# Dividing the attention heads by their softmax sums in the last stage instead of in the head loop, in a fused transformer layer

## What is computed

```
x = x + attention(layernorm(x))          # 16 heads of 64 columns, rotary keys and queries,
x = x + ffn(layernorm(x))                # keys multiplied by a 64x64 matrix a head

# attention, for each batch and each head
sim = q @ k'.T                           # 1024 x 1024
p   = exp(sim - rowmax(sim))
z   = (p @ v) / p.sum(axis=-1)           # the division that the change moves
out = concat(z) @ Wo

# ffn: layernorm, ternary-quantised 256->1024, exact gelu, layernorm, ternary-quantised 1024->256
```

## Time and profile before

| | us |
|---|---|
| median of 3 executions | 3566.96 |
| lowest and highest | 3565.94, 3568.25 |
| span of the profiled execution | 3566.5 |
| TensorE matmul busy | 3472.3 (97%) |
| VectorE busy | 2841.1 (80%) |
| ScalarE busy | 2283.5 (64%) |
| GpSimd busy | 2784.1 (78%) |

### The profile page before, as it was taken

How to read it: one execution, slowest core, us unless ns; L and a number is a source line. 1 busy time by engine, 2 the same in 40 slices (tenths; PEclk the granted TensorE clock), 3 DMA queues, 4 the chain that set the end, 5 groups by cost and what they waited for, 6 DMA issues and landing times. The chain is left out here.

```text
span 3566.5 us, 70837 instructions
## 1 busy us (share of the span) xinstructions
PE 3472.3 (97%) x21150; PEld 2250.9 (63%) x21150; DVE 2841.1 (80%) x4376; ACT 2283.5 (64%) x4340; POOL 2784.1 (78%) x1407
## 2 busy tenths in 40 slices
PE   6999999999999999999999999999999996999999
PEld 4656655665555556555565555566666663888888
DVE  6778777778777777777777777887777777899998
ACT  2666666666666666666666666666666664555555
POOL 2999999999998899999999998999999995222222
PEclk8999999999999999999999999999999998999999
DMA  5222222222222222322222222222222112333332
GB/s 197 84 82 104 88 82 79 78 103 87 87 85 102 85 87 83 106 87 85 82 105 87 87 84 101 87 87 87 104 77 75 59 62 88 92 97 96 97 95 69
DMA packets 219697, 321.71 MB, mean 90 GB/s; under 512 B 20832, under 2 KB 144224, under 8 KB 214880
## 3 DMA queue, kind: packets, MB, share of 16 engines
q1 hardware_dynamic: 210144, 309.28, 25.5%
q10 hardware_dynamic: 9216, 8.39, 0.7%
HBM read 186.52 MB, written 61.60 MB: 70 GB/s over the span
## 5 line engine op out<-in xcount | busy, mean ns | idle before, releaser
L422 POOL TENSOR_TENSOR prob_sum<-prob_sum,prob 128x1024 f32<-128x1024 f32 x762 | 1883.6, 2472 | 248.0 <-ACT prob L506 204.7
L506 ACT ACTIVATE prob<-scores 128x512 f32<-128x512 f32 x2048 | 1072.0, 600 | 572.6 <-PE scores L724 557.8
L654 DVE TENSOR_REDUCE row_max<-max_scores 128x1 f32<-128x512 f32 x1536 | 988.3, 685 | 285.7 <-PE max_scores L773 267.7
L910 PE MATMUL attn_out<-prob,v 128*64 128x512 f32 x4096 | 930.8, 596 | 0.0
L715 PE MATMUL scores<-q_hi,k_hi 64*128 64x512 f32 x2048 | 782.6, 415 | 7.0 <-ACT scores L477 3.9
L724 PE MATMUL scores<-q_lo,k_hi 64*128 64x512 f32 x2048 | 752.8, 393 | 1.3 <-issue 1.3
L720 PE MATMUL scores<-q_hi,k_lo 64*128 64x512 f32 x2048 | 753.5, 394 | 0.0
L910 PEld LDWEIGHTS attn_out<-prob,v 128*64 128x64 f32 x4096 | 285.0, 137 | 557.5 <-issue 556.6
L773 PE MATMUL max_scores<-k_hi,q_hi 64*128 64x512 f32 x1536 | 578.1, 429 | 7.2 <-DVE rows L644 3.0
L477 ACT ACTIVATE scores<-neg_max_seeds 128x512 f32<-128x512 f32 x1024 | 553.3, 603 | 7.6 <-DMA neg_max_seeds<-neg_max_halves 7.6
L715 PEld LDWEIGHTS scores<-q_hi,k_hi 64*128 64x128 f32 x2048 | 376.4, 185 | 275.3 <-issue 159.0
(11 more groups left out here) (137 smaller groups left out, 5005.7 us busy)
## 6 DMA issues: line engine op xcount, KB each, us to landing
rows<-rows SPq DMA_DIRECT2D x512, 128.0 KB, 2.0
neg_max_seeds<-neg_max_halves SPq DMA_DIRECT2D x128, 512.0 KB, 3.8
w_group<-w_parts SPq DMA_DIRECT2D x30, 1536.0 KB, 6.9
attn_normalised<-z_stage SPq DMA_DIRECT2D x128, 256.0 KB, 2.0
v<-attn_normalised SPq DMA_DIRECT2D x64, 512.0 KB, 4.1
x_turned_parts<-x_tile_parts SPq DMA_DIRECT2D x49, 256.0 KB, 3.0
xt_batch<-x_turned_parts SPq DMA_DIRECT2D x7, 1792.0 KB, 11.2
x_in<-in_x SPq DMA_DIRECT2D x64, 128.0 KB, 3.8
```

The lines of the kernel that those rows point to most:

```text
L422: nc.gpsimd.tensor_tensor(psums[half][:, :, :], a, prob[:, n % RING, :, :], ALU.add).then_inc(added, 1)
L506: nc.scalar.activation(prob[:, n % RING, e, :], S[e][n % 2][:, :], ACT.Exp).then_inc(exped[e], 1)
L654: nc.vector.reduce_max(mx[1 - u][:, e, n // 2, n % 2:n % 2 + 1], bank_of(e, jj)[:, :], axis=AX.X)\
L910: nc.tensor.matmul(O[rows(e), :], V[k // 2 % 2][:, j, col:col + DH], prob[:, n % RING, e, :], start=j == 0, stop=j == 7).then_inc(pv_made[ ...
```

## The change

The division leaves the attention loop. Halves of `attn_out` are stored as ScalarE has copied them. The sums are made once a pair, at the end of q = 0 of the next pair, by four products of 32 columns each (two halves, two heads) that fill the four quarters of partitions of `shared`. ScalarE copies the bank to SBUF, SP moves the four rows of 512 into 128x16, VectorE inverts these 2048 values, and SP stores them to HBM. Three `prob_sum` buffers are used in turn in place of two. In the last stage a new station NORM stands between LOAD and SPLIT: SP loads the inverses of the tile spread over 64 partitions for each head of a pair (two DMAs), and GpSimd multiplies the 128x1024 tile by them. The pipeline is one step longer. The diff, cut to its core:

```
-        psums = [sb(f"prob_sum{h}", [P, 2, HALF], F) for h in two]
+        psums = [sb(f"prob_sum{i}", [P, 2, HALF], F) for i in range(3)]
+        sum_rows = sb("sum_rows", [P, HALF], F)
+        sum_cols, inv = (sb(n, [P, 16], F) for n in ("sum_cols", "sum_inverted"))
+        def sums_of(k, half):
+            return psums[(2 * k + half) % 3][:, :, :]
...
         # SP
             def store_z(t, h):
-                wait(sp, z_made, 2 * t + h + 1)
+                wait(sp, z_copied, 2 * t + h + 1)
+            def sum_columns(t):
+                wait(sp, l_copied, t + 1)
+                at_rest()
+                wait(sp, inv_made, t)
+                at_rest()
+                sp.dma_start(sum_cols[:, :], sum_rows[0:P:32, :].rearrange("r (a c) -> r a c", c=16)).then_inc(l_in, 16)
+            def store_inverse(t):
+                wait(sp, inv_made, t + 1)
+                at_rest()
+                sp.dma_start(inv_scr[t].rearrange("h e (a c) -> (h e a) c", c=16), inv[:, :]).then_inc(inv_out, 16)
...
                     for c in two:
                         swap(Q, t, c)
+                if k >= 1:
+                    sum_columns(t - 1)
...
                     max_rows(t, 1)
+                if k >= 1:
+                    store_inverse(t - 1)
                 if attn:
                     store_z(t, 0)
...
             pairs(sp, span)
             store_z(T - 1, 1)
+            sum_columns(T - 1)
+            store_inverse(T - 1)
...
         # GpSimd
                 if j == 1:
-                    wait(pool, l_made, 4 * (t - 1) + 2 * half + 2)
+                    wait(pool, l_made, 4 * (t - 1) + 4 * half)
-            def norm_z(t, h):
-                wait(pool, inv_made, 2 * t + h + 1)
-                wait(pool, z_copied, 2 * t + h + 1)
-                nc.gpsimd.tensor_tensor(zst[h][:, :], zst[h][:, :], inv[:, :], ALU.mult).then_inc(z_made, 1)
-                        if jj == 0 and q == 1 and k >= 1:
-                            norm_z(t - 1, 1)
-                        if jj == 0 and q == 3 and attn:
-                            norm_z(t, 0)
...
         # ScalarE
+            def copy_sums(t):
+                wait(act, l_made, 4 * t + 4)
+                wait(act, l_in, 16 * t)
+                nc.scalar.activation(sum_rows[:, :], M[:, :], ACT.Copy).then_inc(l_copied, 1)
                     if attn and q < 3:
                         seed(t, q + 1)
+                    if q == 0 and k >= 1:
+                        copy_sums(t - 1)
...
         # VectorE
-            def invert(t, h):
-                wait(dve, l_made, 4 * t + 2 * h + 2)
-                wait(dve, z_made, 2 * t + h)
-                nc.vector.reciprocal(inv[:, :], M[:, :]).then_inc(inv_made, 1)
+            def invert(t):
+                wait(dve, l_in, 16 * (t + 1))
+                wait(dve, inv_out, 16 * t)
+                nc.vector.reciprocal(inv[:, :], sum_cols[:, :]).then_inc(inv_made, 1)
-                        if k >= 1:
-                            invert(t - 1, 1)
-                    if q == 2 and attn:
-                        invert(t, 0)
+                    if q == 2 and k >= 1:
+                        invert(t - 1)
...
         # TensorE; its waits on inv_made for the bank become waits on l_copied
-            def sums(t, h, last=False):
-                for e in two:
-                    if last and h:
-                        pe.wait_ge(added_last, 7)
-                    else:
-                        wait(pe, added, 14 * t + 7 * h + 7)
-                    nc.tensor.matmul(M[rows(e), :], ones[:, :], psums[h][:, e, :], start=True, stop=True).then_inc(l_made, 1)
+            def sums(k, t, last=False):
+                if last:
+                    wait(pe, added, 14 * t + 7)
+                    pe.wait_ge(added_last, 7)
+                else:
+                    wait(pe, added, 14 * t + 14)
+                for h in two:
+                    for e in two:
+                        i = 2 * h + e
+                        nc.tensor.matmul(M[32 * i:32 * i + 32, :], ones[:, 0:32], sums_of(k, h)[:, e, :], start=True, stop=True)\
+                            .then_inc(l_made, 1)
-                        if q == 2:
-                            ...
-                            sums(t, 0)
...
     # feed_forward
-        LOAD, SPLIT, Y_MADE, UP, GATE, DOWN, RES = range(7)
+        LOAD, NORM, SPLIT, Y_MADE, UP, GATE, DOWN, RES = range(8)
...
         # SP
                 if at(j, q, LOAD):
                     t, r = at(j, q, LOAD)
+                    wait(sp, z_normed, t - 1)
+                    sp.sem_inc(sp_carrier, 1)
+                    for e in two:
+                        sp.dma_start(zi[r % 2][e * DH:(e + 1) * DH, :, :],
+                                     iv[(t >> 3) & (B - 1), (t >> 2) & 1, e, :, bass.ds((t & 3) * P, P)].partition_broadcast(DH))\
+                            .then_inc(inv_in[r % 2], 16)
                     if q >= 2:
                         wait(sp, z_lo, t - 1)
...
         # GpSimd
-            pool.wait_ge(folded, 3)
             def step(j, q):
+                if q == Y_MADE:
+                    pool.wait_ge(folded, 3)
+                if at(j, q, NORM):
+                    t, r = at(j, q, NORM)
+                    pool.wait_ge(z_in[r % 2], 16 * (t >> 1) + FREE)
+                    pool.wait_ge(inv_in[r % 2], 32 * (t >> 1) + 32)
+                    nc.gpsimd.tensor_tensor(za[r % 2], za[r % 2], zi[r % 2][:, :, :], ALU.mult).then_inc(z_normed, 1)
                 if at(j, q, DOWN):
...
         # ScalarE
                 if at(j, q, SPLIT):
-                    act.wait_ge(z_in[r % 2], 16 * (t >> 1) + FREE)
+                    wait(act, z_normed, t + 1)
```

More of the change, by code:

```diff
@@ L176, in adds_by, with attention @@
     return 7 * (n // 8) + max(n % 8, 1)
-def attention(nc, x, xt_scr, w_scr, z_scr, nm_scr, w_out, late, late_in, stage, XT, W, V, WB, prob, space, ident, gam, alpha, ffn_in, ffn_parts, next_loads):
+def attention(nc, x, xt_scr, w_scr, z_scr, inv_scr, nm_scr, w_out, late, late_in, stage, XT, W, V, WB, prob, space, ident, gam, alpha, ffn_in, ffn_parts, next_loads):
     with ExitStack() as ctx:
@@ L270, in _ @@
         def _(sp):
-            for s in swap_in[K] + swap_in[Q] + z_stored + nm_in + nm_out + seed_in + [x_in] + x_stored:
+            for s in swap_in[K] + swap_in[Q] + z_stored + nm_in + nm_out + seed_in + [x_in, l_in, inv_out] + x_stored:
                 sp.sem_inc(s, CREDIT)
@@ L391, in _ @@
             store_z(T - 1, 1)
+            sum_columns(T - 1)
+            store_inverse(T - 1)
             for h in two:
                 wait(sp, z_stored[h], 16 * T)
+            wait(sp, inv_out, 16 * T)
             for u in two:
@@ L399, in _ @@
         def _(pool):
-            for s in rot_made + [added, z_made, x_rs]:
+            for s in rot_made + [added, x_rs]:
                 pool.sem_inc(s, CREDIT)
@@ L420, in add @@
                     wait(pool, added, 14 * t + adds_by(n - 1))
-                    a = psums[half][:, :, :]
-                nc.gpsimd.tensor_tensor(psums[half][:, :, :], a, prob[:, n % RING, :, :], ALU.add).then_inc(added, 1)
+                    a = sums_of(k, half)
+                nc.gpsimd.tensor_tensor(sums_of(k, half), a, prob[:, n % RING, :, :], ALU.add).then_inc(added, 1)
             def rope(t, x):
@@ L451, in _ @@
             pairs(pool, span)
-            norm_z(T - 1, 1)
         @blk.scalar
         def _(act):
-            for s in exped + hi_made + seeded + [v_copied, nm_hi, z_copied, x_normed, x_hi]:
+            for s in exped + hi_made + seeded + [v_copied, nm_hi, z_copied, l_copied, x_normed, x_hi]:
                 act.sem_inc(s, CREDIT)
@@ L550, in _ @@
             copy_z(T - 1, 1)
+            copy_sums(T - 1)
         @blk.vector
@@ L695, in _ @@
             pairs(dve, span)
-            invert(T - 1, 1)
+            invert(T - 1)
         @blk.tensor
@@ L755, in max_score @@
                     if q == 1 and i == 2:
-                        wait(pe, inv_made, 2 * (t - 1) + 2)
-                    if q == 3 and i == 2:
-                        wait(pe, inv_made, 2 * t + 1)
+                        wait(pe, l_copied, t)
                 elif q and i == 0:
@@ L888, in span @@
                                     wait(pe, x_red[1], 16 * (t + 1) + 2)
-                                wait(pe, inv_made, 2 * (t - 1) + 1)
-                            sums(t - 1, 1)
-                        if q == 2:
-                            if proj:
-                                wait(pe, v_copied, 2 * pp + 1)
-                            else:
-                                if prep:
-                                    wait(pe, x_red[1], 16 * (t + 1) + 10)
-                                wait(pe, inv_made, 2 * (t - 1) + 2)
-                            sums(t, 0)
+                                wait(pe, l_copied, t - 1)
+                            sums(k - 1, t - 1)
                         half = q // 2
```

(16 more changed lines are left out.)

12 lines of the change are left out of this document (7 added, 5 removed).

## The result

The changed kernel takes 3639.97 us (median of 4 runs, 3637.97 to 3643.01) against 3566.45 us before: a ratio of 1.0207, 95% interval 1.0192 to 1.0221. It is slower by 73.5 us; the forecast was 3634. The attention part became shorter, as forecast, and the last stage longer. But the last stage became so in two ways, and the prediction had seen one.

What follows compares the result with a forecast made beforehand. TensorE bounds the attention loop; in the last stage, delaying VectorE by more than 0.28 us lengthens the step. Sum: 3566.5 - 28 (loop) - 8 (way out) + 99 (last stage) + 4 (its start) = 3633.5, forecast 3634 us, range 3592 to 3695.

Steps and rivals of the forecast that it cites:

- q = 2 without sums, four products at once, another arrangement: Attention loop, TensorE: sums leaving q = 2 save 0.85 us a pair; four 32-column products run together, changing arrangement costs 0.1.
- Rival (a): Attention loop, q = 0: the four 32-column products run only two at a time, +53 us, 3687 us; chance 0.17.
- The collision of `q_lo`: Attention loop, q = 1: VectorE's `q_lo` waits behind GpSimd's next addition, ending 1.1 us later; 0.3 us a pair, +19 us.
- Until the last stage: Before the last stage: loop -28 us, last pair and way out -8, start of the last stage +4.
- the start of the stage: Last stage's start: the first two NORM fall among VectorE's ten `ln_shift_wide`; between nothing and 4.8 us, taken as +4.
- The term of +99 us for NORM: Last stage: GpSimd's NORM makes VectorE's `gelu_gained` wait, +1.65 us a step over some 60 steps.
- The rule of exclusion: Last stage: VectorE instructions with two SBUF inputs and GpSimd instructions reading SBUF exclude each other throughout; the same +99 us.
- rival (c): Last stage: GpSimd yields while running, VectorE waits only 0.5 to 1.2 us a step; 3565 to 3607 us; chance 0.09.
- issued ahead of the load, in SP's idle time: Last stage: SP issues the two DMAs of inverses before the load of `v`; no cost, DMA share some 0.5.
- the prediction's sign: Last stage, profile after: `gelu_gained` near 3.2 us instead of 1.28, a step of about 9.8 us.
- the sign of being wrong: Last stage: if `gelu_gained` and `zn_lo` keep 1.28 and 1.22 us, the prediction is wrong by its largest term.
- Rival (b): Last stage: NORM runs in VectorE's gap of over 3 us from `x_gained` to `gelu_gained`, costing nothing; 3531 us; chance 0.10.

Runs made afterwards that it cites:

- the run with neither suspect: Changed kernel with the inverses loaded for the first two tiles only and GpSimd's NORM multiply cut to one column: 3528.55 us, ratio 0.9898.
- the multiply alone: Changed kernel with the inverses loaded for the first two tiles only, GpSimd's NORM multiply kept whole: 3618.08 us, ratio 1.0149.
- the run with the layout alone: Whole changed kernel with inverses stored in HBM tile by tile, a partition's eight pieces side by side as one 4 KB run: 3622.52 us, ratio 1.0159.

## Why the prediction was right, and where it was not

**q = 2 without sums, four products at once, another arrangement: right.** A pair became 0.53 us shorter; forecast were 0.85 - 0.1 - 0.3 = 0.45. With the collision measured at 0.18, the sums and the arrangement together are worth 0.71 against the 0.75 of the prediction. No run parts the two. Rival (a), two products at a time, is refuted by the eight records in 1.07 us. The Trainium skill, page "TensorE: Matmul & The Clock Gate", section "Part 3: Packing small matmuls", gives 2.38 times for three groups; by it some loss was to be expected, and this trace shows none in the records themselves (1.07 us against 1.08).

**The collision of `q_lo`: the mechanism right, the price too high.** It ends 1.08 us after GpSimd, as worked out; what reached the pair was 0.18 us, not 0.3. Over the 62 pairs that is 7 us less than forecast. (The working took 0.55 us for each of two ScalarE instructions for which the earlier trace rows have 0.60; after the change their starts lie 0.50 apart.)

**Until the last stage: right.** Forecast -28 - 8 + 4 = -32 us by the first `x_after_attn`; the trace says -34.8. Two things lie behind this: the loop gave some 5 us more than forecast (62 x 0.53 = 33), and the run with neither suspect is there 39.6 us earlier than before, so the start of the stage costs about 5 us, where 4 were taken.

**The last stage: sum right, half of its cause missing.** The term of +99 us for NORM stands as a price: the multiply alone cost 89.5 and, with the layout changed, 94.5. The rule of exclusion was what the runs showed, and rival (c), that GpSimd yields, fell with `gelu_gained` at 2.9 us. The step that failed is the sentence that the two DMAs of inverses are "issued ahead of the load, in SP's idle time", with a DMA share of some 0.5. The share was right (0.56) and said nothing. The sum put them at nothing. Those loads land after 10.3 us, hold SP's queue, make `v` and `x_in` late, and alone cost 103.5 us. The forecast of 3634 came out at 3640 because the two costs overlap almost wholly, and nothing in the prediction had said so: that it came this close is in good part luck. In the changed kernel GpSimd waits for `v` itself in most steps (192.7 us in 54 waits), so NORM comes late and meets `x_gained` or, rarely, `zn_lo` instead. Only in 17 of 64 steps does `gelu_gained` show the prediction's sign, near 3.2 us; in 47 it keeps the 1.28 us that the prediction had named as the sign of being wrong. The average of 1.75 us hides both, and that was the hint of a second cause.

**Rival (b), NORM in a gap: not what the change does, but what it can be made to do.** The prediction had seen over 3 us there and worked out 3531. With the multiply put there, the loads mended, and the addition moved (0.18 x 62 = 11 us less, 5 more for the longer step), one gets 3525; measured 3526. The agreement is rough: by the first `x_after_attn`, moving the addition gave 8.1 us over the run with the layout alone.

## What to carry to other kernels

Before data are laid into HBM for a later stage, look at how they will be read: in this kernel a load to many partitions from the same addresses became cheap when each partition's share lay in one run. An added load is judged by its landing time and by the duration of its issue against its neighbours', not by the share of busy DMA engines. A free slot on GpSimd counts only where VectorE's instruction at that moment doesn't have two SBUF operands: order the two engines' instructions by a wait. And when a sign in the profile comes out halfway, look at its single steps and not at the average: a second mechanism may lie behind the same time.

## What had not been expected of the hardware

64 partitions reading the same eight scattered pieces of 512 B: 256 KB land in 10.8 us (median) and the issue holds the queue for 1.7 us (up to 4.6). With own rows they take 5.2 and 0.6 us, with one common run of 4 KB 4.9 and 0.5, with two common runs of 2 KB, in the attention loop, 4.1 and 0.65. In the same kernel such loads do little harm in some stretches (7.5 us, issue 0.6) and much in others (12.3 and 2.1), by their place in HBM as it seems. While they do, a load of 512 KB that takes 4.1 us otherwise takes 11.8. Whether the HBM or the DMA engines are held, and whether by the number, the distance or the addresses of the short reads, was not tried.

Four products of 32 columns run on TensorE in the time of two of 64 (eight records in 1.07 us, four in 1.08). And the exclusion of VectorE and GpSimd holds in both directions: a one-column power on GpSimd took 1.52 us instead of 0.55 beside `gelu_gained`. With one of VectorE's operands in PSUM, as for `up_biased`, neither engine held the other (1.40 and 2.40 us side by side).
